# The beginning of a two-layer attention and expert kernel: batch 0's sums before the statistics, its Newton rounds and value scaling on VectorE, smaller loads, later tokens' turns and logits further back

## The reference, cut to what matters

```
mu, var = mean(x), var(x)                       # per token, over 128
xn = (x - mu) * rsqrt(var + 1e-5) * gamma
q = xn @ w_q;  k, v = split(xn @ w_kv)          # 16 heads of 64
k, v = concat(null_k, k), concat(null_v, v)     # 2 null keys a head
q, k = l2norm(q) * q_scale, l2norm(k) * k_scale
sim = 8 * q k^T + alibi, causal;  out = softmax(sim) v @ w_out
logits = layernorm'd tokens @ gate_W + gate_b   # first layer's routing, top 1
out = expert(top1)(tokens);  ...                # then attention and a top-2 mixture of layer 1
```

## Time and profile before

| | us |
|---|---|
| median of three runs (lowest, highest) | 1047.64 (1046.26, 1048.5) |
| span of the profiled execution | 1043.3 |
| PE busy / DVE / ACT / POOL | 961.4 / 692.3 / 630.9 / 650.4 |
| chain that ended last: PE / DVE / ACT / POOL | 54% / 18% / 7% / 7% |
| first product of attention step 0 on PE starts | 63.11 |

### The profile page before, as it was taken

How to read it: one execution, slowest core, us unless ns; L and a number is a source line. 1 busy time by engine, 2 the same in 40 slices (tenths; PEclk the granted TensorE clock), 3 DMA queues, 4 the chain that set the end, 5 groups by cost and what they waited for, 6 DMA issues and landing times.

```text
span 1043.3 us, 21426 instructions
## 1 busy us (share of the span) xinstructions
PE 961.4 (92%) x6330; PEld 690.3 (66%) x6330; DVE 692.3 (66%) x2589; ACT 630.9 (60%) x1945; POOL 650.4 (62%) x803
## 2 busy tenths in 40 slices
PE   5699989999999979999999999999998999999965
PEld 2465546666658976666665665666666788999954
DVE  6988867886673335867768768677885474345634
ACT  4458857667664557677676775766765564444442
POOL 4663787888855544667776678788746651555540
PEclk9889999999999999999999999999999999999997
DMA  9300202202427783033032030331232134787759
GB/s 296 79 7 6 42 27 66 71 26 64 113 74 188 221 233 84 10 72 81 6 66 50 22 71 26 73 67 41 52 82 52 34 102 143 227 229 226 219 168 242
DMA packets 95444, 103.19 MB, mean 99 GB/s; under 512 B 10096, under 2 KB 83031, under 8 KB 95089
## 3 DMA queue, kind: packets, MB, share of 16 engines
q1 hardware_dynamic: 88752, 89.36, 33.5%
q0 software_dynamic: 6592, 12.65, 3.5%
HBM read 77.54 MB, written 23.50 MB: 97 GB/s over the span
## 4 chain that ended last, share of the span: by engine, by line
PE 54%; DVE 18%; ACT 7%; POOL 7%; issue 6%; DMA 3%; SPq 3%; DVEq 0%; POOLq 0%; ACTq 0%
PE bank L1347 9%; PE bank L823 8%; PE bank L834 7%; PE bank L1376 7%; PE bank L1403 5%; DVE arena L2032 5%; PE bank L1391 4%; ACT arena L1759 4%; PE bank L1366 3%; PE bank L1426 3%; DVE arena L2041 3%; POOL arena L1130 2%; DVE arena L1932 2%; POOL expert_rows L655 2%; DMA arena<-in_b 1%
## 5 line engine op out<-in xcount | busy, mean ns | idle before, releaser
L1759 ACT ACTIVATE arena<-arena 128x128 f32<-128x128 f32 (+1 forms) x512 | 226.9, 446 | 96.7 <-DVE arena L2032 96.5
L2032 DVE CUSTOM_DVE_ANT_0 arena<-bank,arena 128x128 f32<-128x128 f32 (+1 forms) x512 | 183.0, 412 | 107.1 <-PE bank L1376 104.4
L1347 PE MATMUL bank<-arena 128*128 128x512 f32 x384 | 211.1, 636 | 6.0 <-ACT arena L1748 3.6
L1130 POOL TENSOR_TENSOR arena<-arena 128x512 f32<-128x512 f32 x128 | 133.4, 1045 | 121.7 <-ACT arena L1735 104.1
L2041 DVE COPY arena<-bank 128x384 f32<-128x384 f32 x256 | 130.0, 549 | 21.1 <-PE bank L1391 20.9
L1145 POOL TENSOR_TENSOR arena<-arena 128x512 f32<-128x512 f32 x128 | 129.5, 1048 | 1.3
L1735 ACT ACTIVATE arena<-bank 128x512 f32<-128x512 f32 x192 | 112.7, 588 | 27.8 <-PE bank L1347 27.5
L1391 PEld LDWEIGHTS bank<-const,arena 128*128 128x128 f32 x768 | 91.3, 142 | 56.0 <-issue 55.0
L784 POOL DMA_INDIRECT expert_out<-arena x71 | 71.1, 1002 | 90.0 <-DVE arena L923 42.1
L1376 PE MATMUL bank<-arena 64*128 64x128 f32 (+1 forms) x1024 | 119.3, 351 | 2.2 <-DVE arena L2032 1.5
L1403 PE MATMUL bank<-arena 128*64 128x256 f32 (+1 forms) x1024 | 112.2, 340 | 9.1 <-DVE arena L2041 8.7
(11 more groups left out here) (304 smaller groups left out, 1634.1 us busy)
## 6 DMA issues: line engine op xcount, KB each, us to landing
arena<-in_wp SPq DMA_DIRECT2D x40, 514.0 KB
arena<-recip_rows SPq DMA_DIRECT2D x30, 512.0 KB, 6.4
XN<-in_wp SPq DMA_DIRECT2D x24, 514.0 KB
arena<-expert_rows SPq DMA_DIRECT2D x46, 129.0 KB, 3.2
arena<-in_b SPq DMA_DIRECT2D x64, 64.0 KB
arena<-expert_out SPq DMA_DIRECT2D x16, 256.0 KB, 5.1
expert_out<-fill SPq DMA_DIRECT2D x11, 338.6 KB, 7.9
expert_rows<-fill SPq DMA_DIRECT2D x1, 2644.5 KB, 21.6
```

The lines of the kernel that those rows point to most:

```text
L1130: pool.tensor_tensor(sq[:, i % 2], r, r, ALU.mult).then_inc(S["sq_done"], 1)
L1347: mm = pe.matmul(RING[bnk][:, :], xa[:, p, t * P:(t + 1) * P], wqkv[:, 512 * k:512 * k + 512], start=True, stop=True)
L1759: ins = act.activation(w, w, ACT.Exp, bias=nm[:, p, 16 * t + h:16 * t + h + 1], scale=-1.0, accum_out=den[:, p, 16 * t + h:16 * t + h + 1])
L2032: ins = v.tensor_tensor_reduce(out=SPb[:, c % 2, 384 * k + P * t:384 * k + P * t + n], in0=SBANK[k][:, P * t:P * t + n], in1=alibi[:, h, N ...
```

## The change

- Loads: the identity is loaded alone ahead of the weights and the rest of the constants behind them; w_k and w_v are two transfers with a semaphore each. PE waits for the identity at the start and for the other constants in `nulls`.
- POOL scales only w_k (two instructions); DVE scales w_v (two instructions) after it has evacuated the first group's turned tokens into `xa`, which ACT did before. ACT begins with a copy of one column, ahead of its first waits.
- DVE: the head scales, the statistics of tiles 4 to 31 and the null keys' norm no longer stand ahead of `sums(0, 0)`. Two `bn_stats` stand behind each of `sums(0, 1)` to `sums(0, 6)`; after `seeds(0)` DVE does the three Newton rounds itself (nine instructions), and POOL only waits for them. Then come the scales, 16 `bn_stats`, `norm_twice` of 28 tiles, `second_norm` of group 1 and now `null_norm`, ahead of `sums(1, 0)`. The groups 5 to 7 are normalised for the second time by ACT (`second_norm_late`), not by DVE. The null scores stand behind `sums(1, 7)`.
- PE: `tokens(1)` stands behind unit 5 of batch 1 and no longer behind unit 2, and the others move back with it; `null_keys`, `tokens(2)`, `logits(1)` are behind unit 6, `null_weights`, `tokens(3)`, `logits(2)` behind unit 7, and behind the ring come tokens 4 to 7, logits 3 to 7, `null_scores(0)` and `scores(0, 0)`.
- ACT: `first_norm` of tiles 0 to 3 moves from ahead of unit 4 to behind unit 11 of batch 0.

The rest of the diff renames semaphores (four new ones, some unused ones dropped). Its core:

```diff
@@ -968,6 +968,7 @@
         xr = RA[:, :].rearrange("p (t d) -> p t d", d=D)
+        LATE = 5
         XPART = (0, 4, 16, NT)
@@ -992,9 +993,11 @@
             sp.dma_start(gamma0, a["L0_attn_gamma"].unsqueeze(1)).then_inc(S["gamma_in"], 16)
-            sp.dma_start(const[:, :], a["const"]).then_inc(S["const_in"], 16)
+            sp.dma_start(ident, a["const"][:, C_ID:C_ID + P]).then_inc(S["ident_in"], 16)
             sp.dma_start(wqkv[:, 0:H * DH], a["L0_attn_w_q"]).then_inc(S["wq_in"], 16)
-            sp.dma_start(wqkv[:, H * DH:3 * H * DH], a["L0_attn_w_kv"]).then_inc(S["wkv_in"], 16)
+            sp.dma_start(wqkv[:, H * DH:2 * H * DH], a["L0_attn_w_kv"][:, 0:H * DH]).then_inc(S["wk_in"], 16)
+            sp.dma_start(wqkv[:, 2 * H * DH:3 * H * DH], a["L0_attn_w_kv"][:, H * DH:2 * H * DH]).then_inc(S["wv_in"], 16)
+            sp.dma_start(const[:, C_ID + P:C_END], a["const"][:, C_ID + P:C_END]).then_inc(S["const_in"], 16)
             sp.dma_start(nkp, a["nkp"]).then_inc(S["nkp_in"], 16)
@@ -1129,12 +1132,14 @@
-            def normalise(a_):
+            def normalise(a_, newton=True):
                 x = xh[:, :, :].rearrange("p t n -> p (t n)")
-                for _ in range(3):
+                if not newton:
+                    pool.wait_ge(S["newton"], (a_ + 1) * 12)
+                for _ in range(3 if newton else 0):
                     for out, i0, i1, op in ((nw1, y, y, ALU.mult), (nw2, nw1, x, ALU.mult),
@@ -1148,12 +1153,12 @@
             pool.wait_ge(S["gamma_in"], 16)
-            pool.wait_ge(S["wkv_in"], 16)
-            for k in range(2, 6):
+            pool.wait_ge(S["wk_in"], 16)
+            for k in range(2, 4):
                 w = wqkv[:, 512 * k:512 * k + 512]
-                pool.tensor_tensor(w, w, gamma0.to_broadcast([P, 512]), ALU.mult).then_inc(S["wkv_scaled"], 1)
+                pool.tensor_tensor(w, w, gamma0.to_broadcast([P, 512]), ALU.mult).then_inc(S["wk_scaled"], 1)
             squares(0, lambda i: ring_use(-1, ("unit", i, 0)))
-            normalise(0)
+            normalise(0, newton=False)
             squares(1, lambda i: ring_use(-1, ("unit", i, 1)))
@@ -1288,7 +1293,10 @@
             def tokens(g):
-                pe.wait_ge(S["xn2_ready"], 4 * g + 4)
+                if g < LATE:
+                    pe.wait_ge(S["xn2_ready"], 4 * g + 4)
+                else:
+                    pe.wait_ge(S["xn2_late"], 4 * (g - LATE) + 4)
                 if g >= 2:
@@ -1334,7 +1342,7 @@
-            pe.wait_ge(S["const_in"], 16)
+            pe.wait_ge(S["ident_in"], 16)
             tokens(0)
@@ -1508,6 +1516,7 @@
+                pe.wait_ge(S["const_in"], 16)
                 pe.wait_ge(S["w_in"], 16 * 2)
@@ -1534,29 +1543,35 @@
                     k = UNITS[use[1]][1]
-                    pe.wait_ge(S["wq_scaled" if k < 2 else "wkv_scaled"], k % 2 + 1 if k < 2 else k - 1)
+                    pe.wait_ge(S[("wq_scaled", "wk_scaled", "wv_scaled")[k // 2]], k % 2 + 1)
                 if use == ("qk", 0, 0):
                     u = use[1]
-                    if u == NQ - 1:
-                        pe.wait_ge(S["ring_evac"], ring_use(-1, ("qk", NQ - 1, 0)) + 1)
-                        scores(0, 0)
                     if u == 0:
                         logits(0)
-                    if u >= 2:
-                        tokens(u - 1)
-                    if u >= 3:
-                        logits(u - 2)
-                    if u == 4:
+                    if u == 5:
+                        tokens(1)
+                    if u == 6:
                         null_keys()
-                    if u == 5:
+                        tokens(2)
+                        logits(1)
+                    if u == 7:
                         null_weights()
-                    if u == 6:
-                        pe.wait_ge(S["wn_evac"], 1)
-                        null_scores(0)
+                        tokens(3)
+                        logits(2)
+            tokens(4)
+            logits(3)
+            pe.wait_ge(S["wn_evac"], 1)
+            null_scores(0)
+            tokens(5)
+            logits(4)
+            pe.wait_ge(S["ring_evac"], ring_use(-1, ("qk", NQ - 1, 0)) + 1)
+            scores(0, 0)
+            tokens(6)
+            logits(5)
             tokens(7)
@@ -1703,6 +1718,8 @@
+            act.wait_ge(S["ones_ready"], 1)
+            act.activation(small[:, 5:6], ones[:, 0:1], ACT.Copy)
             act.wait_ge(S["gamma_in"], 16)
@@ -1711,10 +1728,13 @@
                 act.wait_ge(S["tok2_T"], g + 1)
-                dst = RA[:, 512 * g:512 * g + 512] if g else xa[:, :, :].rearrange("p i n -> p (i n)")
-                act.activation(dst, TBANK[g % 2][:, :], ACT.Copy).then_inc(S["tok2_evac"], 1)
-
-            tokens_out(0)
+                act.activation(RA[:, 512 * g:512 * g + 512], TBANK[g % 2][:, :], ACT.Copy).then_inc(S["tok2_evac"], 1)
+
+            def second_norm_late(g):
+                act.wait_ge(S["stats_ready"], 2)
+                for i in range(4 * g, 4 * g + 4):
+                    act.activation(XN2[i], RS_[:, i], ACT.Identity, bias=NMR2[:, 1, i:i + 1], scale=RSTD2[:, 1, i:i + 1])\
+                       .then_inc(S["xn2_late"], 1)
@@ -1799,8 +1819,6 @@
             for use in RING_FIRST:
-                if use == ("unit", 4, 0):
-                    first_norm(act, 0, 4, 1)
                 if use == ("qk", 0, 0):
@@ -1809,9 +1827,13 @@
                 ring_out(use, ring_use(-1, use), ring_bank(-1, use), use[2])
-                if use[0] == "unit" and use[2] == 1 and use[1] >= 2:
-                    tokens_out(use[1] - 1)
-            tokens_out(7)
+                if use == ("unit", NU - 1, 0):
+                    first_norm(act, 0, 4, 1)
+                if use[0] == "unit" and use[2] == 1 and use[1] >= 5:
+                    second_norm_late(use[1])
+                    tokens_out(use[1] - 4)
+            for g in range(4, 8):
+                tokens_out(g)
             for k in range(2):
@@ -1950,11 +1972,18 @@
             second_norm(v, 0, 4, 1)
-            v.wait_ge(S["scales_in"], 64)
-            link(v.tensor_scalar(T1[:, 0:1], qscale, kscale, 8.0, ALU.mult, ALU.mult))
-            v.tensor_copy(qscale, T1[:, 0:1]).then_inc(S["scale_ready"], 1)
-            v.wait_ge(S["scale_ready"], 1)
-            v.wait_ge(S["x_in1"], 16)
+            v.wait_ge(S["tok2_T"], 1)
+            v.tensor_copy(xa[:, :, :].rearrange("p i n -> p (i n)"), TBANK[0][:, :]).then_inc(S["tok2_evac"], 1)
+            v.wait_ge(S["gamma_in"], 16)
+            v.wait_ge(S["wv_in"], 16)
+            for k in range(4, 6):
+                w = wqkv[:, 512 * k:512 * k + 512]
+                v.tensor_scalar(w, w, gamma0, None, ALU.mult).then_inc(S["wv_scaled"], 1)
+            def scales():
+                v.wait_ge(S["scales_in"], 64)
+                link(v.tensor_scalar(T1[:, 0:1], qscale, kscale, 8.0, ALU.mult, ALU.mult))
+                v.tensor_copy(qscale, T1[:, 0:1]).then_inc(S["scale_ready"], 1)
+                v.wait_ge(S["scale_ready"], 1)
             def null_norm():
@@ -1964,20 +1993,31 @@
-            for i in range(4, 16):
-                v.bn_stats(ST6[:, i], RS_[:, i])
-            null_norm()
             for i in range(NQ):
                 sums(0, i)
-                if i >= 2:
-                    if i == 2:
-                        v.wait_ge(S["x_in2"], 16)
-                    for j in range(3 * i + 10, min(3 * i + 13, NT)):
-                        ins = v.bn_stats(ST6[:, j], RS_[:, j])
+                if i == 1:
+                    v.wait_ge(S["x_in1"], 16)
+                if 1 <= i < NQ - 1:
+                    for j in range(2 * i + 2, 2 * i + 4):
+                        v.bn_stats(ST6[:, j], RS_[:, j])
             seeds(0)
+            v.wait_ge(S["seed_done"], 1)
+            y, half, t1 = (m[:, :, :].rearrange("p t n -> p (t n)") for m in (rn, xh, ss))
+            for i in range(3):
+                link(v.tensor_tensor(t1, y, half, ALU.mult))
+                link(v.tensor_tensor(t1, t1, y, ALU.mult))
+                ins = v.scalar_tensor_tensor(out=y, in0=t1, scalar=1.5, in1=y, op0=ALU.add, op1=ALU.mult)
+                if i < 2:
+                    link(ins)
+            ins.then_inc(S["newton"], 12)
+            scales()
+            v.wait_ge(S["x_in2"], 16)
+            for j in range(16, NT):
+                ins = v.bn_stats(ST6[:, j], RS_[:, j])
             link(ins)
             second_norm(v, 4, 4, 2)
+            null_norm()
@@ -1988,7 +2028,9 @@
             v.tensor_copy(nvw, MISC[0:R, P:2 * P]).then_inc(S["nv_evac"], 1)
-            second_norm(v, 8, 8, 2)
+            sums(1, 0)
+            second_norm(v, 8, 4, 2)
+            sums(1, 1)
@@ -2158,21 +2200,17 @@
             SUMS = {2: (0,), 3: (1,), 4: (2, 3), 5: (4, 5), 6: (6, 7)}
-            sums(1, 0)
+            second_norm(v, 12, 4, 2)
+            sums(1, 2)
+            null_evac()
             second_norm(v, 16, 4, 2)
-            sums(1, 1)
```

(13 more changed lines are left out.)

6 lines of the change are left out of this document (3 added, 3 removed).

## The result

The changed kernel is slower: 1055.26 us median of six runs (1053.64 to 1057.06), beside 1047.71 for six of the kernel before (1046.26 to 1050.1). The ratio is 1.0088, 95% interval [1.0066, 1.011]. The prediction was 1054.0 with the range 1043.5 to 1057.0. The profiled span is 1053.6 us, 10.3 longer than in the earlier trace rows; why that is more than the 7.6 between the medians is told under "The sum".

What follows compares the result with a forecast made beforehand. PE's order of work was taken to set the end. Step 0 starting 7.4 us later, less 1.0 relief, gave +6.4: span 1049.7, median 1054.0 from 1047.64. Range 1043.5 to 1057.

Steps and rivals of the forecast that it cites:

- The sum: Whole kernel: +7.4 at step 0's start and -1.0 relief give +6.4, a span of 1049.7 and a median of 1054.0.
- Part 1, loads and first unit: Start to GpSimd's scaling of batch 0: first unit at 12.4, scaling at 27.9 (bounds 26.6 to 29.6), 6.0 earlier.
- The hold-up of 1.2: VectorE's four early second normalisations, beside GpSimd's two w_k products: late by 0 to 1.5 us, taken 1.2.
- Part 2, VectorE's row: VectorE behind the scaling's start: group 1's second normalisation ends at 40.8 against 43.05, group 2's at 47.5.
- Part 3, PE's row and the clock: PE from tokens(1) to step 0: low clock from the null weights adds 10.1; start taken at 70.5, +7.4.
- The wait behind unit 6: PE behind unit 6 stands some 4.4 us for VectorE's tokens(2), with one small turn in them.
- my upper case, 71.9: Step 0's first product starts at 71.9 if PE's clock is low from unit 7 on.
- Rival (1): PE ahead of step 0: clock holds or returns at once, step 0 at 61.0, 1044.5 us; chance 0.24.
- Rival (2): PE's row: logits and null weights do not slow at low clock; step 0 at 64.6, 1048.1 us; chance 0.11.
- Rival (3): Early part: no early gain, clock full, step 0 at 63.1, within 1 of before; chance 0.05.
- Relief in step 0: Step 0: GpSimd's batch 1 Newton and scaling come earlier, holding up 0 to 3 us less of VectorE; taken -1.0.
- VectorE beside GpSimd: By the skill's page, VectorE's PSUM evacuation of `xa`, sums and `bn_stats` are free of GpSimd's hold; no row showed the copy.

Runs made afterwards that it cites:

- e1: Changed kernel with the null keys' norm moved to where VectorE waits for the first sum: 1049.61 us, 1.0042 of before.
- e2: Changed kernel with five extra unread 128x512 products on PE, in the two gaps and ahead of the null weights: 1051.18 us, 1.0045 of before.
- e4: Kernel before with only the change's PE order of turns, logits and null products, and ACT's order to match: 1054.12 us, 1.0067 of before.
- e3: Changed kernel with ten extra unread products on PE, in all gaps and through the row of turns and logits: 1053.07 us, 1.006 of before.
- e5: Changed kernel's early part with null keys' norm early, then the kernel before's order on PE, ACT and VectorE: 1047.17 us, 1.0013 of before.
- e7: Changed kernel, null keys' norm and null products early, tokens(1) to tokens(4) earlier, logits(3) ahead of unit 7, two extra PE products: 1043.8 us, 0.9973 of before.
- e10: The kernel of e7 unchanged, run again on another occasion: 1045.3 us, 1.0001 of the kernel before.

## Why the prediction was right

**Part 1, loads and first unit.** In the profiled execution, too pessimistic: w_k landed near 9.0, not 8.3, so GpSimd's two products began when VectorE's four normalisations were nearly done (8.03 to 9.15). The hold-up of 1.2 did not occur, and the first unit started at 11.16, not 12.4. But that is one execution. e1's agrees with it (9.03, and PE's first turn at 9.33), while in the seven other traces with these loads GpSimd begins at 8.38 to 8.76 and PE's first turn comes at 9.79 to 10.70 instead of 9.30: there the hold-up that I forecast is real, 0.5 to 1.4 us, and the first unit starts at 11.66 to 12.57. Sum and seeds behind the last square took 1.5 (23.20 to 24.70), Newton 2.4 instead of 1.9, just above my bound of 2.3 (nine of 0.23 with 0.26 from start to start). Scaling began at 27.22, not 27.9, within the bounds.

**Part 2, VectorE's row.** The end, 40.97 for 40.8, is right by luck. The row of short instructions began at 32.64 and not at 34.2: the scaling had begun 0.7 earlier, and the scales, done before it, took 0.4 instead of 1.2. From there I took the one-operand instructions as free of the hold (five in 1.0) and three of the two-operand ones as held (ten in 4.5). The five `tensor_scalar` ran under GpSimd's multiplication from 32.64 to 37.31 and took 0.67 to 1.08 each, 4.7 in all; the ten two-operand ones came when GpSimd was through, at 0.22 each, 2.5 in all. So the row was 1.7 longer than forecast, and this made up for its start 1.6 earlier. Both kinds are held beside 128x512 multiplications: before, a two-operand one took 1.09 there (33.96). The null keys' norm behind it took 3.2, as forecast; groups 2 and 3 came at 45.33 and 47.74.

**Part 3, PE's row and the clock.** The wait behind unit 6 was 1.98 + 2.10 against 4.4. The null weights' records took 3.41 against 3.4. The clock fell at 46.8, ahead of `tokens(2)`, `logits(1)` and unit 7, and not with the null weights at 50.9; that is earlier than in my upper case, 71.9, which had it low from unit 7. The scores still came at 71.44 against 70.5 taken. Turn, logits and unit 7 took 4.3 instead of 2.1, but the wait of 1.3 for `null_evac` that I had behind them did not occur, as VectorE was done with it at 50.33 and PE came to it at 51.59. The row behind the null weights took 16.6 (54.86 to 71.44), as forecast at half speed. The mechanism as I put it was only half of it: I named the idle stretch as the point from which it is decided, and e2 and e4 show that without it the row alone lowers the clock, at 56.1 and 57.7 instead of 46.8. The end would have been nearly the same without the idle stretch (e4: 1.0067), so the forecast was right also by what it named only in passing, that turns and logits alone had been granted 0.50. Rival (1), that the clock holds, would not have come true without the gap either, and e3, where it did hold with extra work, did not give its 1044.5. Rival (2) falls with the loads at 333 ns. The Trainium skill's rule in "TensorE: Matmul & The Clock Gate", "LDWEIGHTS", columns over 1.2 GHz, gives 107 ns for 128 columns at either clock, an estimate from that page; the loads here took 190 to 192 and 332 to 337 ns, and the measurement decides. Rival (3), no early gain, is wrong at GpSimd and right at the scores (e5: 0.8 of 6).

**Relief in step 0.** Mis-sized: taken -1.0, measured -0.2 from first to fourth scores (11.43 after, 11.65 before). GpSimd's Newton rounds of batch 1 wait for the null scores' chain on VectorE, which moved back as well, and its scaling ran to 75.24, still beside step 0. VectorE's four instructions of the first logits cost 1.67 (0.64, 0.19, 0.42, 0.42) instead of 2.28. Why only 0.2 of these 0.6 is seen at the fourth scores no run tells; PE's low clock there, to 77.5, is the likely reason.

**The sum.** +6.4 forecast, +7.6 between the medians, +10.3 between the profiled executions. Most of the difference between the last two is the choice of executions. In every run on record that gives both, the time is 1.8 to 1.9 above the span. So the 4.3 us that I took above as lying around the span are 1.9 around it and some 2.4 by which the profiled execution of before was faster than the median; that of after (1055.51) was not. In the traces, 8.1 of the 10.3 stand at the fourth scores. Some 1.5 more come near 153 us, where behind the same wait for VectorE (2.76 us after, 2.75 before) the clock is low for 6.8 us instead of 3.4. As such drops differ between executions of one kernel (e7 and e10), this part is not shown to be a property of the change.

**VectorE beside GpSimd.** The Trainium skill's rule in "SBUF — State Buffer", "Who interferes with whom", held for the copy from PSUM (0.69 at 10.42, beside GpSimd's second product) and for the sums (0.69 from 18.20 on, beside the squares; the sum at 27.58 that the prediction names for this lies behind the last square of the earlier trace rows). It does not free `tensor_scalar`: the same section counts it among the instructions that can enter the two-port modes, and the five above, which I had taken as free, were held. But beside GpSimd's Newton rounds (128x64) the same five took 0.17 to 0.19 in the kernel before, while two-operand ones took 0.34 to 0.38:

```profile
31.30 0.19 DVE L355 TENSOR_SCALAR arena<-arena 128x56 int32<-128x56 int32 x1
31.98 0.38 DVE L359 TENSOR_TENSOR arena<-arena 128x56 f32<-128x56 f32 x1
```

## What to carry to other kernels

Before moving work off one engine, ask which engine the next consumer waits for: 6 us won on GpSimd became 0.8 at the scores (e5), because the work went to VectorE, and VectorE's tokens were what PE lacked. Small products (turns, eight-column logits) kept the full clock while they lay between large ones in the kernel before; collected into a row of their own they lowered TensorE's clock even where it never waited (e4), and then the whole row cost double. Read the granted clock beside the idle times, and price a low stretch by what comes next: in PE's own row it doubled every item, where VectorE is due anyway (start of step 0) it cost under 1 us. And look at more than one execution: what one trace shows of the clock, or of a load's arrival, another of the same kernel may not.

## What the runs showed of the hardware

- The clock fell in rows without a gap: e2 from 56.1, with PE busy 12.65 of the 13.1 us before; e4 from 57.7, 11.95 of 12.7. It did not fall in 45 to 59.1 before, with units and qk in between, PE busy 13.47 of 14.1. One kernel did both: e7 fell at 51.3, with PE busy 5.86 of the 6.3 us before, and e10 kept 1.00 there, with 5.61 of 6.3.
- `tensor_scalar` of 128x28 and 128x56 (float and int32) took 0.67 to 1.08 beside GpSimd's 128x512 multiplications and 0.17 to 0.19 beside its 128x64 ones, while `bn_stats` and `bn_aggr` kept their 0.2 and 1.95 and the sums their 0.66 to 0.69. A `scalar_tensor_tensor` of 32x1 took 0.93 beside GpSimd instead of 0.15 (e1, 15.43 us).
- One program's clock falls at different places from run to run (51.3 and 68.3 us in e7 and e10), and its time goes with it: over 30, 33 and 23 runs of the kernel before, mean granted clock and time are correlated by -0.74, -0.70 and -0.78. Of the 23, the twelve at 0.986 or more have a median of 1043.8 us, the six at 0.983 or less 1048.6.
